# Post-norm attention and ternary FFN layer on eight cores: four 128x128 transposes to a PSUM bank instead of one, and two sets of squaring tiles

## The chip, the cores and the metric

The kernel runs on the 8 cores of one Trainium2 chip, one batch element of 2048 tokens by 2048 features on each core, with no traffic between the cores. The metric is the device time of the slowest core in microseconds. The profile is that of core 0, the slowest in the profiled execution.

## The reference

```python
x = _layernorm(x + attn(x, w_qkv, b_qkv, w_out, b_out))     # x: (8, 2048, 2048) float32
x = _layernorm(x + ffn(x, w_fc, w_proj))
# attn: one head of width 2048
#   qkv = x @ w_qkv.T + b;  scores = q @ k.T / sqrt(2048);  probs = softmax(scores)
#   out = (probs @ v) @ w_out.T + b_out
# ffn:  h = square(relu(x @ ternary(w_fc).T));  out = h @ ternary(w_proj).T     # hidden width 5120
```

Every float32 operand of a matmul is split into a bf16 high part and a bf16 low part (the rest). A product of two split matrices is three bf16 matmuls; one with a ternary matrix is two.

## The kernel before

The program is written out by hand as a list of instructions for each engine. `B.op` appends an instruction to an engine's list with the semaphore values that it waits for; each instruction of VectorE, ScalarE and GpSimd also waits for the completion of the one before it on its own engine. So each engine works its list strictly in order.

First come the transposes of x (L337 to L344) and then the QKV projection (L484) with the ternary quantization of the FFN weights beside it. The V part of this stage ends in `v_emit`: four transposes (L439) of 128x128 into the four quarters of one PSUM bank, then four 128-column evictions on each of ScalarE (L445) and VectorE (L452).

Then four groups `g` of 512 tokens run one after the other, each through these stages:

1. scores: matmuls L649, copies of 8 PSUM banks to `sco` (L667, L671);
2. softmax and the transposes of the probabilities, for each of 4 row tiles `qt` (a row tile is 128 tokens): row maximum (L690), bias (L694), exponential with the row sum (L697), reciprocal (L702), normalization (L704), then 16 steps `kc`, each with one float32 transpose of 128x128 on TensorE (L710) into the first 128 columns of PSUM bank 0 or 1 in turn, a ScalarE copy of these to bf16 in `pth` (L714), and a VectorE subtraction for the low part in `ptl` (L718), which frees the bank;
3. probabilities times V: matmuls L760, evictions L773 and L777;
4. output projection: matmuls L831, L842, L845, residual added by L849;
5. first layer norm, for each of 4 row tiles `sci`: sum (L861), sum of squares (L866), small steps (L864 to L880), application (L882), then again 16 steps of transpose (L900), high part (L904, in `y1fh`) and low part (L907, in `y1fl`), with PSUM banks 0 and 1 in turn;
6. first FFN product: 40 accumulations of 32 matmuls (L939); after each, relu into `rl` (L947, ScalarE), its square into `t2` (L950, VectorE), the high part of it (L952, ScalarE) and the low part (L954, VectorE). There is one tile `rl` and one tile `t2`;
7. second FFN product: matmuls L999, evictions L1014, and a second layer norm with the store.

The matmuls of stage 3 wait for the last low part of stage 2 (`t_pt_done[-1]`), those of stage 6 for the last low part of stage 5 (`t_y1_tr[-1]`), and those of stage 7 for the last low part of stage 6 (`t_hsq_done[-1]`). No matmul of another stage is queued between the transposes. A stretch of 16 transposes with their evictions is called a unit below: 4 groups with 4 row tiles at two places make 32 units.

Of the kernel before, what the change touches and what calls it, by code (L numbers as in the profile page):

```python
# [7 lines left out]
AL = mybir.AluOpType  # L8
AF = mybir.ActivationFunctionType
# [84 lines left out]
def build_core():  # L94
# [46 lines left out]
    pb = [nc.alloc_psum_tensor("pb%d" % i, [128, 512], F32).ap() for i in range(8)]  # L141

    B = Builder(nc)
# [26 lines left out]
    for c, v in ((C2048, 2048.0), (CN, 10485760.0), (C7, 7.0), (C10, 10.0),  # L170
# [46 lines left out]
    tern_scale = {}  # L217
# [356 lines left out]
    pth = bb(PTH, 8192)  # L574
# [9 lines left out]
    y1fh = bb(Y1FH, 8192)  # L584
    y1fl = bb(Y1FL, 8192)
    qfcs = bb(QFCS, 8192)
    rl = bf(RL, 512)
    t2 = bf(T2, 512)
# [4 lines left out]
    for g in range(4):  # L593
        s30 = s3_end if g == 0 else []

        def ge(*keys):
            return [grp_end[k] for k in keys]
# [90 lines left out]
        for qt in range(4):  # L688
            pnb = pn2[qt % 2]
            t_nm = B.op("vector", lambda e, qt=qt: e.tensor_reduce(  # L690
                vcol(NMAX), sco[:, qt * 2048:(qt + 1) * 2048], axis=AX.X, op=AL.max,
                negate=True), waits=sco_qt_toks[qt] + [pn_norm[qt % 2]],
                inc="sV")
            t_eb = B.op("vector", lambda e: e.tensor_tensor(  # L694
                vcol(EBIAS), vcol(NMAX), vcol(SSCB), op=AL.mult),
                waits=[t_sscb], inc="sV")
            t_exp = B.op("scalar", lambda e, qt=qt, pnb=pnb: e.activation(  # L697
                pnb, sco[:, qt * 2048:(qt + 1) * 2048], AF.Exp,
                bias=vcol(EBIAS), scale=vcol(SSCB), accum_out=vcol(ESUM)),
                waits=[t_eb, pn_read[qt % 2]] + (ge("pe") if qt == 0 else []),  # L700
                inc="sA")
            t_rq = B.op("vector", lambda e: e.reciprocal(vcol(RQ), vcol(ESUM)),  # L702
                        waits=[t_exp], inc="sV")
            t_pn = B.op("vector", lambda e, pnb=pnb: e.tensor_single_scalar(  # L704
                pnb, pnb, vcol(RQ), op=AL.mult),
                waits=[t_rq], inc="sV")
            pn_norm[qt % 2] = t_pn
            for kc in range(16):
                bk = kc % 2
                t_tr = B.op("tensor", lambda e, kc=kc, bk=bk, pnb=pnb: e.transpose(  # L710
                    pb[bk][:, 0:128], pnb[:, kc * 128:(kc + 1) * 128], idn),
                    waits=[t_pn, bank_free[bk]], inc="sP")
                dst = kc * 512 + qt * 128
                t_hi = B.op("scalar", lambda e, bk=bk, dst=dst: e.activation(  # L714
                    pth[:, dst:dst + 128], pb[bk][:, 0:128], AF.Copy),
                    waits=[t_tr] + (ge("out0", "out1") if qt == 0 and kc == 0 else []),
                    inc="sA")
                t_lo = B.op("vector", lambda e, bk=bk, dst=dst: e.tensor_tensor(  # L718
                    ptl[:, dst:dst + 128], pb[bk][:, 0:128], pth[:, dst:dst + 128],
                    op=AL.subtract), waits=[t_tr, t_hi], inc="sV")  # L720
                bank_free[bk] = t_lo
                t_pt_done.append(t_lo)
            pn_read[qt % 2] = t_tr
# [162 lines left out]

        t_y1_tr = []
        t_ln_prev = None
        for sci in range(4):
            y_toks = [y_map[(sci, oh_, os_)] for oh_ in range(2) for os_ in range(2)]  # L890
            t_ap, _ = layer_norm(
                yb[:, sci * 2048:(sci + 1) * 2048],
                y1b[:, sci * 2048:(sci + 1) * 2048],
                y_toks + [t_qsl_lastread if sci == 0 else None],
                sci, dump_extra=t_y_done[-1] if sci == 0 else None)
            t_ln_prev = t_ap
            for dc in range(16):
                bk = (sci * 16 + dc) % 2
                src_off = sci * 2048 + dc * 128
                t_tr = B.op("tensor", lambda e, src_off=src_off, bk=bk: e.transpose(  # L900
                    pb[bk][:, 0:128], y1b[:, src_off:src_off + 128], idn),
                    waits=[t_ap, bank_free[bk]], inc="sP")
                dst = dc * 512 + sci * 128
                t_hi = B.op("scalar", lambda e, bk=bk, dst=dst: e.activation(  # L904
                    y1fh[:, dst:dst + 128], pb[bk][:, 0:128], AF.Copy),
                    waits=[t_tr], inc="sA")
                t_lo = B.op("vector", lambda e, bk=bk, dst=dst: e.tensor_tensor(  # L907
                    y1fl[:, dst:dst + 128], pb[bk][:, 0:128], y1fh[:, dst:dst + 128],
                    op=AL.subtract), waits=[t_tr, t_hi], inc="sV")
# [5 lines left out]
        t_rl_free = None  # L915
        t_t2_free = None
        for hcb in range(10):
            t_qld = []
            for dc in range(16):
                t_qld.append(B.dma(qfcs[:, dc * 512:(dc + 1) * 512],  # L920
                             qfc[dc * 128:(dc + 1) * 128, hcb * 512:(hcb + 1) * 512],
                             waits=[t_qf_free if dc == 0 else None,
                                    t_d_lastmm if hcb == 0 and dc == 0 else None] +
                             (tern_done[0] if g == 0 and hcb == 0 and dc == 0 else []),
                             stream="ts%d" % dc))
            t_mmf = {}
            for h4 in range(4):
                bk = h4 + 4 * (hcb % 2)
                n_mm = 0
                for dc in range(16):  # L930
                    for amat in (y1fh, y1fl):
                        first = (n_mm == 0)
                        last = (n_mm == 31)
                        w = []
                        if first:
                            w = [t_y1_tr[-1], bank_free[bk]]
                        if h4 == 0 and amat is y1fh:
                            w = list(w) + [t_qld[dc]]
                        t_mmf[bk] = B.op("tensor", lambda e, dc=dc, h4=h4, amat=amat, bk=bk, first=first, last=last: e.matmul(  # L939
                            pb[bk], qfcs[:, dc * 512 + h4 * 128: dc * 512 + h4 * 128 + 128],  # L940
                            amat[:, dc * 512:(dc + 1) * 512],
                            start=first, stop=last),
                            waits=w, inc="sP" if last else None)
                        n_mm += 1
                hca = hcb * 4 + h4
                hoff = hsq_off(hca)
                t_rl = B.op("scalar", lambda e, bk=bk: e.activation(  # L947
                    rl, pb[bk], AF.Relu, scale=vcol(SFCB)),
                    waits=[t_mmf[bk], tern_scale[0], t_rl_free], inc="sA")
                t_t2 = B.op("vector", lambda e: e.tensor_tensor(t2, rl, rl, op=AL.mult),  # L950
                            waits=[t_rl, t_t2_free], inc="sV")
                t_hi = B.op("scalar", lambda e, hoff=hoff: e.activation(  # L952
                    bb(hoff, 512), t2, AF.Copy), waits=[t_t2], inc="sA")
                t_lo = B.op("vector", lambda e, hoff=hoff: e.tensor_tensor(  # L954
                    bb(hoff + 1024, 512), t2, bb(hoff, 512), op=AL.subtract),
                    waits=[t_hi], inc="sV")
# [120 lines left out]
```

How the kernel before makes its waits and increments, by code:

```python
                    def run(eng):  # L78
                        satisfied = {}
                        for fn, ws, inc in self.ops[eng_name]:
                            for sname, v in ws:
                                if satisfied.get(sname, -1) >= v:
                                    continue
                                eng.wait_ge(handles[sname], v)
                                satisfied[sname] = v
                            ins = fn(eng)
                            if inc is not None:
                                ins.then_inc(handles[inc[0]], inc[1])
```

## Time and profile before

| | us |
|---|---|
| median of the 2 timed runs | 8209.84 (7855.29 and 8564.4) |
| profiled execution, device time | 7726.85 |
| its span on core 0 | 7724.7 |
| spans of its other cores | 7624.6 to 7713.0 |
| TensorE busy on core 0 | 6804.0 (88%) |
| VectorE, ScalarE busy | 1320.9 (17%), 1549.1 (20%) |

The span runs from a core's first instruction to its last. The profiled execution is shorter than both timed runs; a saving found in the trace is one of microseconds in that execution.

### The profile page before, as it was taken

The page shows a single profiled execution, that of the slowest core. Times are in us where ns is not written, and L with a number is a line of the kernel's source. Part 1 is how long each engine was busy: PE and PEld are TensorE (multiplying, and loading weights), DVE is VectorE, ACT ScalarE, POOL GpSimd, SP SyncE. Part 2 cuts the span into 40 slices and gives each one's busy share as a digit, 9 for nine tenths or more (in the row PEclk, how much of TensorE's full clock was granted, in tenths as well). Part 3 has the DMA queues.
Part 4 walks back from the last instruction along what each step waited for, and adds up shares of the span by engine and source line. Part 5 has one row for each costly group of instructions (what it writes and reads, how often), then busy time and mean ns, then how long its engine had stood idle before and what let it go on. Part 6 is the DMA issues. An engine that isn't in the chain of part 4 may idle for free.

```text
span 7724.7 us, 82337 instructions; the slowest of 8 cores (7624.6 to 7724.7 us)
## 1 busy us (share of the span) xinstructions
PE 6804.0 (88%) x29840; PEld 3014.2 (39%) x29840; DVE 1320.9 (17%) x2408; ACT 1549.1 (20%) x2523; POOL 259.3 (3%) x499
## 2 busy tenths in 40 slices
PE   5999998899998798899779799987979998797998
PEld 2344443344444343334334333433433443343343
DVE  3111244312221201210110211011021000202101
ACT  3333566612221101210110111011021000102100
POOL 0111122200000000000000000000000000000000
PEclk9888999999999798899879799997979999797999
DMA  2556777713333132122313112231312223131222
GB/s 99 149 158 175 203 233 235 228 63 94 95 100 106 60 118 79 51 62 75 119 58 119 64 55 69 76 123 58 117 50 66 70 73 129 59 116 46 66 71 82
DMA packets 394272, 785.58 MB, mean 102 GB/s; under 512 B 105105, under 2 KB 219793, under 8 KB 381585
## 3 DMA queue, kind: packets, MB, share of 16 engines
q1 hardware_dynamic: 334994, 570.59, 23.2%
q0 software_dynamic: 58880, 209.75, 9.5%
q8 instruction: 243, 3.98, 0.2%
q14 instruction: 155, 1.27, 0.1%
HBM read 654.34 MB, written 125.83 MB: 101 GB/s over the span
## 4 chain that ended last, share of the span: by engine, by line
PE 77%; ACT 7%; DVE 7%; issue 3%; DMA 3%; SPq 1%; DVEq 0%; ACTq 0%; POOL 0%; POOLq 0%
PE pb L484 20%; PE pb L939 14%; PE pb L999 14%; PE pb L649 9%; PE pb L831 9%; PE pb L760 8%; DVE ab L280 2%; ACT af L274 2%; ACT af L278 2%; DMA ab<-qfc 1%; SPq L61 1%; ACT af L882 1%; PE pb L710 1%; PE pb L337 1%; PE pb L900 1%
## 5 line engine op out<-in xcount | busy, mean ns | idle before, releaser
L484 PE MATMUL pb<-ab,ab 128*128 128x512 bf16 x9216 | 2113.3, 394 | 59.6 <-ACT af L278 44.7
L484 PEld LDWEIGHTS pb<-ab,ab 128*128 128x128 bf16 x9216 | 927.2, 101 | 1220.5 <-issue 379.2
L939 PE MATMUL pb<-ab,ab 128*128 128x512 bf16 x5120 | 1177.1, 390 | 102.0 <-DMA ab<-qfc 95.0
L999 PE MATMUL pb<-ab,ab 128*128 128x512 bf16 x5120 | 1118.3, 381 | 18.8 <-DVE ab L954 14.8
L939 PEld LDWEIGHTS pb<-ab,ab 128*128 128x128 bf16 x5120 | 497.6, 100 | 780.7 <-issue 270.7
L649 PE MATMUL pb<-ab,ab 128*128 128x512 bf16 x3072 | 672.0, 382 | 139.6 <-DMA ab<-qf 139.6
L999 PEld LDWEIGHTS pb<-ab,ab 128*128 128x128 bf16 x5120 | 499.2, 98 | 637.8 <-issue 53.6
L831 PE MATMUL pb<-ab,ab 128*128 128x512 bf16 x3072 | 680.7, 385 | 26.5 <-DVE ab L777 14.1
L760 PE MATMUL pb<-ab,ab 128*128 128x512 bf16 x3072 | 672.0, 382 | 4.6 <-DVE ab L718 4.6
L649 PEld LDWEIGHTS pb<-ab,ab 128*128 128x128 bf16 x3072 | 302.0, 98 | 509.3 <-issue 153.2
L831 PEld LDWEIGHTS pb<-ab,ab 128*128 128x128 bf16 x3072 | 303.4, 99 | 404.0 <-issue 53.3
L760 PEld LDWEIGHTS pb<-ab,ab 128*128 128x128 bf16 x3072 | 302.2, 98 | 373.6 <-issue 17.3
L866 ACT ACTIVATE af<-af 128x2048 f32<-128x2048 f32 x32 | 61.1, 1910 | 1867.7 <-DVE af L1014 1122.8
L900 PE MATMUL pb<-idn,af 128*128 128x128 f32 x256 | 105.7, 444 | 216.3 <-ACT af L882 141.1
L947 ACT ACTIVATE af<-pb,st 128x512 f32<-128x512 f32 x160 | 110.0, 687 | 913.6 <-PE pb L939 913.6
L710 PE MATMUL pb<-idn,af 128*128 128x128 f32 x256 | 105.7, 444 | 206.8 <-DVE af L704 130.4
L950 DVE TENSOR_TENSOR af<-af 128x512 f32<-128x512 f32 x160 | 110.7, 692 | 913.4 <-ACT af L947 913.4
L280 DVE TENSOR_TENSOR ab<-af,af 128x1024 bf16<-128x1024 f32 x160 | 196.0, 1225 | 385.9 <-ACT af L278 325.2
L1014 DVE SCALAR_TENSOR_TENSOR af<-pb,st,af 128x512 f32<-128x512 f32 x64 | 48.0, 750 | 1091.6 <-PE pb L999 1085.8
L274 ACT ACTIVATE af<-af,st 128x1024 f32<-128x1024 f32 x160 | 183.7, 1148 | 211.0 <-DVE ab L280 210.3
L495 ACT ACTIVATE ab<-pb,bqkv_sb 128x512 bf16<-128x512 f32 x128 | 88.0, 687 | 517.6 <-PE pb L484 507.7
L337 PE MATMUL pb<-idn,af 128*128 128x128 f32 x256 | 108.7, 446 | 91.7 <-DVE ab L344 84.0
(89 smaller groups left out, 2628.5 us busy)
## 6 DMA issues: line engine op xcount, KB each, us to landing
af<-wfct POOLq DMA_DIRECT2D x160, 512.0 KB, 5.5
af<-wprt POOLq DMA_DIRECT2D x160, 512.0 KB, 6.0
ab<-qfc SPq DMA_DIRECT2D x640, 128.0 KB, 2.9
ab<-qpr SPq DMA_DIRECT2D x320, 256.0 KB, 2.7
ab<-kf SPq DMA_DIRECT2D x128, 512.0 KB, 3.3
ab<-vt SPq DMA_DIRECT2D x128, 512.0 KB, 3.3
ab<-wos SPq DMA_DIRECT2D x128, 512.0 KB, 3.3
af<-wqk SPq DMA_DIRECT2D x48, 1024.0 KB, 6.7
```

Source lines behind the costliest of these rows:

```text
L274: t_s1 = B.op("scalar", lambda e, b=buf, tc=NTHRv: e.activation(tz_ta, b, AF.Sign, bias=vcol(tc)), waits=[load_tok[k], t_q] + (stats[wi] i ...
L278: t_s2 = B.op("scalar", lambda e, b=buf, tc=THRv: e.activation(tz_tb, b, AF.Sign, bias=vcol(tc)), inc="sA")
L280: t_q = B.op("vector", lambda e, qb=qb: e.tensor_tensor(qb, tz_ta, tz_tb, op=AL.add), waits=[q_free[qsl_], t_s2], inc="sV")
L337: t_tr = B.op("tensor", lambda e, xr=xrow, hc=hc, bk=bk: e.transpose(pb[bk][:, 0:128], xr[:, hc * 128:(hc + 1) * 128], idn), waits=[t_ld, ...
L484: t_mm = B.op("tensor", lambda e, a=a, bmat=bmat, hc=hc, ss=ss, bk=bk, first=first, last=last: e.matmul(pb[bk], a[:, hc * 128:(hc + 1) * 128],
L649: t_hcmm = B.op("tensor", lambda e, a_off=a_off, b_off=b_off, bk=bk, kb=kb, first=first, last=end_of_acc: e.matmul(pb[bk], qsl[:, a_off:a_ ...
L710: t_tr = B.op("tensor", lambda e, kc=kc, bk=bk, pnb=pnb: e.transpose(pb[bk][:, 0:128], pnb[:, kc * 128:(kc + 1) * 128], idn), waits=[t_pn, ...
L760: t_last = B.op("tensor", lambda e, vbuf=vbuf, a_off=a_off, kc=kc, pmat=pmat, bk=bk, first=first, last=end_of_acc: e.matmul(pb[bk], vbuf[: ...
L831: t_last = B.op("tensor", lambda e, amat=amat, coff=coff, wbuf=wbuf, b_off=b_off, bk=bk, first=first: e.matmul(pb[bk], amat[:, coff:coff + ...
L900: t_tr = B.op("tensor", lambda e, src_off=src_off, bk=bk: e.transpose(pb[bk][:, 0:128], y1b[:, src_off:src_off + 128], idn), waits=[t_ap, ...
L939: t_mmf[bk] = B.op("tensor", lambda e, dc=dc, h4=h4, amat=amat, bk=bk, first=first, last=last: e.matmul(pb[bk], qfcs[:, dc * 512 + h4 * 12 ...
L999: t_last = B.op("tensor", lambda e, a_ap=a_ap, sci=sci, qpb=qpb, ds=ds, bk=bk, first=first, last=end_of_acc: e.matmul(pb[bk], a_ap[:, sci ...
```

## The change

In stages 2 and 5 the 16 steps become 4. Each step now makes four transposes into the four quarters of one PSUM bank, with one wait ahead of the first and one semaphore increment behind the last. One ScalarE copy and one VectorE subtraction then take all 512 columns; in `pth`, `ptl`, `y1fh` and `y1fl` they write four runs of 128 elements that lie 512 elements apart. The banks are still 0 and 1 in turn. In stage 6, `rl` and `t2` each get a second tile, at byte offsets 32768 and 34816 (inside `yb`, in the rows of the first row tile), used in turn; the first two relus wait for VectorE's last step of the first layer norm's first row tile as well.

```diff
-    RL, T2 = 163840, 165888
+    RLS = [163840, 32768]
+    T2S = [165888, 34816]
...
-            for kc in range(16):
-                bk = kc % 2
-                t_tr = B.op("tensor", lambda e, kc=kc, bk=bk, pnb=pnb: e.transpose(
-                    pb[bk][:, 0:128], pnb[:, kc * 128:(kc + 1) * 128], idn),
-                    waits=[t_pn, bank_free[bk]], inc="sP")
...
+            for kc4 in range(4):
+                bk = kc4 % 2
+                t_tr = None
+                for j in range(4):
+                    kc = kc4 * 4 + j
+                    t_tr = B.op("tensor", lambda e, kc=kc, j=j, bk=bk, pnb=pnb: e.matmul(
+                        pb[bk][:, j * 128:(j + 1) * 128],
+                        pnb[:, kc * 128:(kc + 1) * 128], idn,
+                        start=(j == 0), stop=(j == 3), is_transpose=True),
+                        waits=[t_pn, bank_free[bk]] if j == 0 else (),
+                        inc="sP" if j == 3 else None)
+                dsth = pth.rearrange("p (kc c) -> p kc c", c=512)[
+                    :, kc4 * 4:kc4 * 4 + 4, qt * 128:qt * 128 + 128]
+                dstl = ptl.rearrange("p (kc c) -> p kc c", c=512)[
+                    :, kc4 * 4:kc4 * 4 + 4, qt * 128:qt * 128 + 128]
+                t_hi = B.op("scalar", lambda e, bk=bk, dsth=dsth: e.activation(
+                    dsth, pb[bk], AF.Copy),
...
+                t_lo = B.op("vector", lambda e, bk=bk, dsth=dsth, dstl=dstl: e.tensor_tensor(
+                    dstl, pb[bk], dsth, op=AL.subtract),
+                    waits=[t_tr, t_hi], inc="sV")
                 bank_free[bk] = t_lo
...
+                pi = hca % 2
+                rl = rls[pi]
+                t2 = t2s[pi]
...
-                    waits=[t_mmf[bk], tern_scale[0], t_rl_free], inc="sA")
+                    waits=[t_mmf[bk], tern_scale[0], t_rl_free[pi]] +
+                    ([ln1_vtok[0]] if hca < 2 else []), inc="sA")
...
-                t_rl_free = t_t2
-                t_t2_free = t_lo
+                t_rl_free[pi] = t_t2
+                t_t2_free[pi] = t_lo
```

The edit of stage 5 is the same as that of stage 2, with `y1b`, `y1fh` and `y1fl` in place of `pnb`, `pth` and `ptl`.

## Rows read from the trace of the kernel before

**Rows 1.** Spans and mean granted TensorE clock by core and die:

```profile
core 0: 7724.7 us, clock 0.921
...
die 1 (median of its cores): 7634.8 us, clock 0.933
```

**Rows 2.** The page's chain that ended last, shares of the span by line:

```profile
PE pb L484 20%; PE pb L939 14%; PE pb L999 14%; PE pb L649 9%; PE pb L831 9%; PE pb L760 8%; DVE ab L280 2%; ACT af L274 2%; ACT af L278 2%; DMA ab<-qfc 1%; SPq L61 1%; ACT af L882 1%; PE pb L710 1%; PE pb L337 1%; PE pb L900 1%
```

**Rows 3.** The chain in order of time, first group: start us, us, what:

```profile
2616.36 0.46 PE pb L710
2617.84 0.46 PE pb L710
...
2628.59 2.30 DVE st L690
...
2635.35 0.46 PE pb L710
...
2686.34 164.26 PE pb L760 x753
...
3049.12 0.46 PE pb L900
...
3061.42 2.30 DVE st L861
```

**Rows 4.** Timeline, first unit: start us, us, engine line op, [idle before, releaser]:

```profile
2616.36 0.66 PE L710 MATMUL pb<-idn,af 128*128 128x128 f32 x2 [9.12 <-DVE af L704]
...
2617.84 0.84 PE L710 MATMUL pb<-idn,af 128*128 128x128 f32 x2 [0.82 <-DVE ab L718]
...
2618.44 0.67 ACT L714 ACTIVATE ab<-pb 128x128 bf16<-128x128 f32 x2 [0.84 <-PE pb L710]
2618.89 0.69 DVE L718 TENSOR_TENSOR ab<-pb,ab 128x128 bf16<-128x128 f32 x2 [0.80 <-ACT ab L714]
...
2619.33 0.84 PE L710 MATMUL pb<-idn,af 128*128 128x128 f32 x2 [0.65 <-DVE ab L718]
```

**Rows 5.** Groups by line: count, busy us, mean ns, idle before and releasers:

```profile
L900 PE MATMUL pb<-idn,af 128*128 128x128 f32 x256 | 105.7, 444 | 216.3 <-ACT af L882 141.1 <-DVE ab L907 75.1
L710 PE MATMUL pb<-idn,af 128*128 128x128 f32 x256 | 105.7, 444 | 206.8 <-DVE af L704 130.4 <-DVE ab L718 76.3
...
L718 DVE TENSOR_TENSOR ab<-pb,ab 128x128 bf16<-128x128 f32 x256 | 74.6, 291 | 124.8 <-ACT ab L714 108.6 <-PE pb L710 3.6 <-DVE ab L718 0.6
...
L714 ACT ACTIVATE ab<-pb 128x128 bf16<-128x128 f32 x256 | 71.1, 278 | 148.3 <-PE pb L710 134.6 <-ACT ab L714 0.4
```

**Rows 6.** The same view, instructions with 512 and 2048 columns:

```profile
L385 ACT ACTIVATE ab<-af 128x2048 bf16<-128x2048 f32 x48 | 91.7, 1910 | 6.8 <-DMA af<-wqk 2.5
...
L849 DVE TENSOR_TENSOR af<-pb,af 128x512 f32<-128x512 f32 x64 | 44.3, 692 | 692.1 <-PE pb L845 686.3
```

**Rows 7.** Timeline of TensorE, four transposes of L439 between matmuls of L484:

```profile
1745.31 0.60 PE L439 MATMUL pb<-idn,af 128*128 128x128 f32 x4
...
1745.75 10.52 PE L484 MATMUL pb<-ab,ab 128*128 128x512 bf16 x48
```

**Rows 8.** Stretches of core 0: busy us of each engine, granted clock, DMA share, GB/s:

```profile
2628.50:2686.00 57.50, 19.70 (x48) 8.50 (x48) 25.58 (x60) 19.88 (x54) 0.00 (x0) 0.50 0.00 1
2686.00:2690.00 4.00, 3.66 (x10) 1.36 (x11) 0.09 (x1) 0.00 (x0) 0.00 (x0) 0.56 0.00 0
2690.00:2696.00 6.00, 6.00 (x30) 2.74 (x28) 0.00 (x0) 0.00 (x0) 0.00 (x0) 1.00 0.25 87
...
3049.00:3119.00 70.00, 26.31 (x64) 11.42 (x64) 28.35 (x85) 30.93 (x76) 0.00 (x0) 0.50 0.00 1
```

**Rows 9.** Groups by line for the squaring chain and the matmuls behind it:

```profile
L999 PE MATMUL pb<-ab,ab 128*128 128x512 bf16 x5120 | 1118.3, 381 | 18.8 <-DVE ab L954 14.8 <-DVE af L1014 2.8 <-DMA ab<-qpr 0.9
...
L954 DVE TENSOR_TENSOR ab<-af,ab 128x512 bf16<-128x512 f32 x160 | 110.8, 693 | 153.8 <-ACT ab L952 153.8
L950 DVE TENSOR_TENSOR af<-af 128x512 f32<-128x512 f32 x160 | 110.7, 692 | 913.4 <-ACT af L947 913.4
...
L947 ACT ACTIVATE af<-pb,st 128x512 f32<-128x512 f32 x160 | 110.0, 687 | 913.6 <-PE pb L939 913.6
...
L952 ACT ACTIVATE ab<-af 128x512 bf16<-128x512 f32 x160 | 100.7, 629 | 162.8 <-DVE af L950 162.8
```

**Rows 10.** Stretches of core 0 in the QKV stage, columns as in Rows 8:

```profile
400.00:600.00 200.00, 193.59 (x737) 80.78 (x736) 28.97 (x73) 69.71 (x110) 24.83 (x48) 0.81 0.58 161
...
2000.00:2200.00 200.00, 200.00 (x966) 95.78 (x964) 41.21 (x85) 48.52 (x105) 0.00 (x0) 1.00 0.35 94
```

More of the change, by code:

```diff
@@ L707, in build_core @@
             pn_norm[qt % 2] = t_pn
-            for kc in range(16):
-                bk = kc % 2
-                t_tr = B.op("tensor", lambda e, kc=kc, bk=bk, pnb=pnb: e.transpose(
-                    pb[bk][:, 0:128], pnb[:, kc * 128:(kc + 1) * 128], idn),
-                    waits=[t_pn, bank_free[bk]], inc="sP")
[L713 to L716, printed above, removed]
+            for kc4 in range(4):
[15 more added lines that the diff above has]
+                    dsth, pb[bk], AF.Copy),
+                    waits=[t_tr] + (ge("out0", "out1") if qt == 0 and kc4 == 0 else []),
                     inc="sA")
-                t_lo = B.op("vector", lambda e, bk=bk, dst=dst: e.tensor_tensor(
-                    ptl[:, dst:dst + 128], pb[bk][:, 0:128], pth[:, dst:dst + 128],
-                    op=AL.subtract), waits=[t_tr, t_hi], inc="sV")
+                t_lo = B.op("vector", lambda e, bk=bk, dsth=dsth, dstl=dstl: e.tensor_tensor(
+                    dstl, pb[bk], dsth, op=AL.subtract),
+                    waits=[t_tr, t_hi], inc="sV")
                 bank_free[bk] = t_lo
@@ L888, in build_core @@
         t_ln_prev = None
+        ln1_vtok = [None] * 4
         for sci in range(4):
@@ L895, in build_core @@
                 sci, dump_extra=t_y_done[-1] if sci == 0 else None)
+            ln1_vtok[sci] = _
             t_ln_prev = t_ap
[L897 to L909, printed above, removed]
+            for dc4 in range(4):
+                bk = (sci * 4 + dc4) % 2
+                t_tr = None
+                for j in range(4):
+                    src_off = sci * 2048 + (dc4 * 4 + j) * 128
+                    t_tr = B.op("tensor", lambda e, src_off=src_off, j=j, bk=bk: e.matmul(
+                        pb[bk][:, j * 128:(j + 1) * 128],
+                        y1b[:, src_off:src_off + 128], idn,
+                        start=(j == 0), stop=(j == 3), is_transpose=True),
+                        waits=[t_ap, bank_free[bk]] if j == 0 else (),
+                        inc="sP" if j == 3 else None)
+                dsth = y1fh.rearrange("p (dc c) -> p dc c", c=512)[
+                    :, dc4 * 4:dc4 * 4 + 4, sci * 128:sci * 128 + 128]
+                dstl = y1fl.rearrange("p (dc c) -> p dc c", c=512)[
+                    :, dc4 * 4:dc4 * 4 + 4, sci * 128:sci * 128 + 128]
+                t_hi = B.op("scalar", lambda e, bk=bk, dsth=dsth: e.activation(
+                    dsth, pb[bk], AF.Copy), waits=[t_tr], inc="sA")
+                t_lo = B.op("vector", lambda e, bk=bk, dsth=dsth, dstl=dstl: e.tensor_tensor(
+                    dstl, pb[bk], dsth, op=AL.subtract),
+                    waits=[t_tr, t_hi], inc="sV")
                 bank_free[bk] = t_lo
@@ L914, in build_core @@
         t_qf_free = None
-        t_rl_free = None
-        t_t2_free = None
+        t_rl_free = [None, None]
+        t_t2_free = [None, None]
         for hcb in range(10):
@@ L946, in build_core @@
                 hoff = hsq_off(hca)
-                t_rl = B.op("scalar", lambda e, bk=bk: e.activation(
+                pi = hca % 2
+                rl = rls[pi]
+                t2 = t2s[pi]
+                t_rl = B.op("scalar", lambda e, bk=bk, rl=rl: e.activation(
                     rl, pb[bk], AF.Relu, scale=vcol(SFCB)),
-                    waits=[t_mmf[bk], tern_scale[0], t_rl_free], inc="sA")
-                t_t2 = B.op("vector", lambda e: e.tensor_tensor(t2, rl, rl, op=AL.mult),
-                            waits=[t_rl, t_t2_free], inc="sV")
-                t_hi = B.op("scalar", lambda e, hoff=hoff: e.activation(
+                    waits=[t_mmf[bk], tern_scale[0], t_rl_free[pi]] +
+                    ([ln1_vtok[0]] if hca < 2 else []), inc="sA")
+                t_t2 = B.op("vector", lambda e, rl=rl, t2=t2: e.tensor_tensor(
+                    t2, rl, rl, op=AL.mult),
+                    waits=[t_rl, t_t2_free[pi]], inc="sV")
+                t_hi = B.op("scalar", lambda e, hoff=hoff, t2=t2: e.activation(
                     bb(hoff, 512), t2, AF.Copy), waits=[t_t2], inc="sA")
-                t_lo = B.op("vector", lambda e, hoff=hoff: e.tensor_tensor(
+                t_lo = B.op("vector", lambda e, hoff=hoff, t2=t2: e.tensor_tensor(
                     bb(hoff + 1024, 512), t2, bb(hoff, 512), op=AL.subtract),
```

4 lines of the change are left out of this document (2 added, 2 removed).

## The prediction

> **What bounds the kernel now.** I read the spans by core first: core 0 is the slowest, die 1 is some 1% shorter at a slightly higher clock [rows 1], so an interval of core 0 stands for all. The chain that ended last belongs to matmuls for the most part [rows 2]: the six large matmul lines have 74% of the span, and the change touches none of them. L710 and L900 have 1% each there, but this understates them, because a unit's chain goes round TensorE, ScalarE and VectorE and only the TensorE piece bears that name. The chain in order of time shows a unit whole. In the softmax it runs from the first transpose at 2616.36 to 2628.59, where VectorE begins the next row tile: 12.23 us; in the layer norm from 3049.12 to 3061.42, 12.30 us [rows 3]. Nothing else runs beside it: the DMA share is 0.00 in both stretches [rows 8], and the matmuls of the next stage wait for the last low part. So 32 units, about 32 x 12.2 = 390 us, 5% of the span, lie bare on the path.
>
> Within a unit the timeline shows a ring of two banks. A pair of transposes starts at 2617.84, the next at 2619.33 [rows 4]: 1.49 us for each of 8 pairs. Its steps are 0.60 us from a transpose's start to its copy's start (2617.84 to 2618.44), 0.45 us from there to the subtraction's start (2618.89), of which 0.278 us is the copy [rows 5] and 0.17 us the hand-over, then 0.291 us of subtraction [rows 5], and 0.15 us until TensorE starts again. TensorE's own work is not the limit; four hand-overs and two short evictions are.
>
> **The change part by part.** It removes 12 of 16 ScalarE copies and 12 of 16 VectorE subtractions in each unit, and adds 384 columns to each of the others. The transposes are as many as before.
>
> The copy: 0.278 us for 128 columns from PSUM [rows 5]. For the slope I take a plain copy to bf16 without pointer operands from SBUF: 0.629 us for 512 columns (L952) [rows 9] and 1.910 us for 2048 (L385) [rows 6], so 1.281 / 1536 = 0.834 ns a column. That gives 0.278 + 384 x 0.000834 = 0.598 us. The nearest upper row is L947, from PSUM with a pointer scale, 0.687 us [rows 9]. I take 0.60.
>
> The subtraction: L849 reads 512 columns of PSUM and as many of SBUF in 0.692 us [rows 6]; I take 0.69. That the four runs of 128 lie 512 elements apart is shown by no row; the least it can cost is nothing, and I take that, since 128 elements in a run is what each instruction writes now.
>
> Four transposes in a row: with the clock at its low level (0.50 through both stretches [rows 8], 1.2 GHz) a pair that nobody holds up lasts 0.66 us, one lasts 0.444 [rows 4, 5], so the second starts 0.21 us behind the first. At the high level L439 starts four in 1745.75 - 1745.31 = 0.44 us [rows 7], 0.11 each; twice that is the same 0.21 or so. So a burst occupies TensorE for 4 x 0.21 = 0.85 us, and the copy starts 0.60 + 3 x 0.21 = 1.24 us behind the first transpose. The other end, in case weight load and matmul don't overlap beyond the first pair, is 0.43 us each, about a transpose's recorded duration of 0.444.
>
> One unit, from its first transpose at 0: T0 0, copy 1.24 to 1.84, subtraction 2.01 to 2.70, bank free and T2 starts 2.85. T1 starts at 0.85, copy 2.09 to 2.69, subtraction 2.86 to 3.55, T3 starts 3.70. T2's copy is at 4.09 to 4.69, its subtraction 4.86 to 5.55. T3's copy is at 4.94 to 5.54, its subtraction 5.71 to 6.40. The next row tile's VectorE work starts 0.10 later, at 6.50, against 12.23: 5.73 us saved. With 32 units that is 183 us. I don't count the 12.30 of the layer norm, nor the shorter distance between the last transposes and the next matmul.
>
> What comes next after a unit is unchanged: from 2628.59 to the next unit's first transpose at 2635.35 TensorE waits 6.76 us for the serial softmax steps, which depend on data and keep their place. So the stretch stays bare. Nothing is late in its place: the DMA queues are idle there [rows 8], and the V rows for L760 and the weights for L939 have landed before the stretches begin.
>
> A rule of the Trainium skill bears on the copy (page "VectorE: DVE Perf Modes", section "The TRN2 errata"): it gives ScalarE from PSUM (172 + columns) cycles at 1.2 GHz, which is 250 ns for 128 columns where the row shows 278, and 570 ns for 512, an estimate from that page. With it a unit would be some 0.06 us shorter and the sum about 2 us larger; the sum goes by the rows.
>
> The two squaring sets: the chain of an accumulation is 0.687 + 0.692 + 0.629 + 0.693 = 2.70 us plus hand-overs, and ScalarE sits idle for 913.6 / 160 = 5.7 us before each L947, waiting for TensorE [rows 9]. With one tile or two, `rl` is long free when the next accumulation ends. I cost this at 0; what hides it is the accumulation's own matmuls. If that cover were gone, it would be the end of the stage, where L999 waits 14.8 / 4 = 3.7 us for L954 [rows 9]: that is the one last chain, whose steps depend on each other, and a second tile doesn't shorten it. A gain is excluded there, and a loss too, as the added wait on the first layer norm is over some 60 us before the first relu, and on ScalarE nothing else is queued.
>
> Sum: 7726.85 - 183 = 7544 us against the profiled execution's own time, 2.4% less. The timed runs shown are longer, median 8209.84, so the same execution's level is 6% under them. The same 183 us off that median would give 8027, and 2.2%.
>
> **The rivals.**
>
> A, transposes that don't stream at 0.21. At 0.43 us each, copies start 1.88 behind the first transpose, a burst takes 1.71, T2 starts at 3.49, T3 at 5.20, the last subtraction ends 5.20 + 1.88 + 0.60 + 0.17 + 0.69 = 8.54. The saving is 3.59 a unit, 115 us: 7612, within 2%. For it: no row shows more than two in a row at the low clock, and the recorded duration is 0.444. Against it: L439's four in 0.44 us. Dearer strided writes would have a like effect: 0.7 us more in each unit is enough to fall below 2%.
>
> B, the clock comes up within a unit. It rises about 4 us into L760's dense matmuls and stands at 1.00 in the next stretch, after 0.50 through the transposes [rows 8], where TensorE started two of 0.21 in each 1.49 us. Now four of 0.21 stand in each 1.4 us or so. At 2.4 GHz I estimate a burst's copy to start 0.48 us sooner: 3 x 0.10 for the spacing, and some 0.17 for the last transpose (0.60 - 3 x 0.11 = 0.27 in place of 0.444 [rows 5, 7]). Once in each unit (T2 and T3 only) that is 15 us; the eight matmul stages behind then don't start with 4 us at half speed, 8 x 2 = 16 us more. That gives 7544 - 31 = 7513. If every burst were fast, the unit would be 5.55 and the whole saving 226: 7501. Against it: 7 us without transposes still lie between units.
> The Trainium skill (page "TensorE: Matmul & The Clock Gate", section "The HAM clock gate") states that the clock rises on sustained activity and falls after idleness; by that rule too the outcome hangs on how full the bursts are, and the trace agrees on the rise of about 4 us.
>
> C, slower: the chip grants less clock elsewhere. Between 400 and 600 us core 0 has 0.81, and only 737 matmuls are done there against 966 at 1.00 [rows 10]. If units that are denser made this state hold in the matmul stages as well, each microsecond of dense matmul would cost 1 / 0.81 - 1 = 0.23 more. It eats the 183 us from 183 / 0.23 = 800 us of such matmuls on, and gives over 2% slower from 1470 us on: 7544 + 0.23 x 1500 = 7889. For it: the state is there in this execution. Against it: it is not there in any of the four groups, where the change is.
>
> D, nothing: each burst waits for the one before it to be evicted whole, and a unit is 4 x 2.85 = 11.4 us, with 0.8 saved in each: 7700. Against it: pairs overlap now, with the same two banks.
>
> **How the numbers follow.** Forecast 0.58, A with its like 0.20, B 0.13, C 0.05, D 0.04. 2% is about what a measurement of this kernel can tell from no change, 155 us here. The forecast lies only 28 us beyond that line, so a tenth of it counts as within 2%: faster 0.52 + 0.13 = 0.65, same 0.06 + 0.24 = 0.30, slower 0.05. In the profiled execution's terms the range is 7500 (B at its full) to 7612 (A), and that is the forecast's own range. Executions of one kernel differ more than that: the timed runs of before lie at 7855 and 8564. A time taken as their median was would be 8027 with the forecast. The stated range reaches from 7490 to 8040 to hold both.
>
> **What the profile would show.** The step L710 to L690 in the chain goes from 12.23 to 6.5 us; 64 copies of 128x512 at each place take 598 ns each (right) or 687; 64 subtractions take 692 ns; four transposes start within 0.64 us of each other (right) or 1.3 (A); the granted clock in the two stretches is 0.50 (right) or above 0.6 (B); L999 still waits about 15 us for L954. The prediction is wrong if matmul stages change their granted clock, or if writes in four runs cost more than writes in one.

## The result

Over all executions the changed kernel has a median of 8125.93 us (11 executions, 7462.28 to 8562.94) and the kernel before one of 8450.11 us (10, 7646.0 to 8742.89). Put against each other without the executions in which a die was held at a lower TensorE clock for a long time, the ratio is 0.977 with a 95% interval of 0.970 to 0.984: 2.3% less time. The interval lies wholly below 1, so the gain is real; a gain of a little under 2% is not excluded by it. The forecast was 2.4% less. The time of 8125.93 lies above the stated range of 7490 to 8040.

The profiled execution of the changed kernel took 7472.31 us, 72 us less than the 7544 forecast for it. Its spans by core (from first to last instruction, with the mean granted clock):

```profile
core 0: 7455.0 us, clock 0.945
...
core 7: 7470.8 us, clock 0.942
die 0 (median of its cores): 7448.2 us, clock 0.945
die 1 (median of its cores): 7458.9 us, clock 0.943
```

Against [rows 1] core 0 is 270 us shorter but die 1 only 176 us. The difference between these two is not the change: in the profile of before core 0 had a granted clock of 0.81 for 481 us of its QKV matmuls ([rows 10] show a part of them), and in this one it had none of that. At 0.81 instead of 1.00 some 90 of these 481 us are lost, which is about the 94 us of difference.

A unit in the changed kernel, from the timeline of core 7 (start us, us, engine line op, idle before and releaser). L714 are the transposes, L724 the copies, L728 the subtractions, L691 the next row tile's maximum:

```profile
2542.67 1.94 PE L714 MATMUL pb<-idn,af 128*128 128x128 f32 x8 [9.12 <-DVE af L705]
2543.91 0.60 ACT L724 ACTIVATE ab<-pb 128x512 bf16<-128x512 f32 x1 [3.22 <-PE pb L714]
2544.68 0.69 DVE L728 TENSOR_TENSOR ab<-pb,ab 128x512 bf16<-128x512 f32 x1 [2.27 <-PE pb L714]
2544.76 0.60 ACT L724 ACTIVATE ab<-pb 128x512 bf16<-128x512 f32 x1 [0.26 <-PE pb L714]
...
2545.51 1.94 PE L714 MATMUL pb<-idn,af 128*128 128x128 f32 x8 [0.90 <-DVE ab L728]
...
2548.38 0.69 DVE L728 TENSOR_TENSOR ab<-pb,ab 128x512 bf16<-128x512 f32 x1 [0.16 <-DVE ab L728]
2549.17 2.29 DVE L691 TENSOR_REDUCE st<-af 128x1 f32<-128x2048 f32 x1
```

The first copy starts 1.24 us behind the first transpose, the third burst 2.84 us behind the first, and the next row tile's work at 6.50 us, where the ring of [rows 3, 4] had 12.23. The first layer norm has the same shape: 2959.29 to 2965.79, 6.50 us too, against 12.30.

The groups by line of the changed kernel (count, busy us and mean ns, idle before and releasers) that answer to [rows 5, 6, 9]:

```profile
L1023 PE MATMUL pb<-ab,ab 128*128 128x512 bf16 x5120 | 1114.4, 380 | 19.3 <-DVE ab L978 14.8 <-DVE af L1038 2.8 <-DMA ab<-qpr 1.3
...
L914 PE MATMUL pb<-idn,af 128*128 128x128 f32 x256 | 62.1, 424 | 164.6 <-ACT af L892 150.1 <-DVE ab L926 14.5
L714 PE MATMUL pb<-idn,af 128*128 128x128 f32 x256 | 62.1, 424 | 153.3 <-DVE af L705 138.5 <-DVE ab L728 14.8
...
L728 DVE TENSOR_TENSOR ab<-pb,ab 128x512 bf16<-128x512 f32 x64 | 44.3, 692 | 61.5 <-PE pb L714 51.8 <-ACT ab L724 4.8 <-DVE ab L728 4.5
...
L724 ACT ACTIVATE ab<-pb 128x512 bf16<-128x512 f32 x64 | 38.2, 597 | 81.1 <-PE pb L714 80.6
```

TensorE's idle time for a bank (behind L728 and L926) went from 76.3 and 75.1 us to 14.8 and 14.5. The wait of the second FFN product for the last low part is 14.8 us, as before.

The granted clock in the first group's two stretches and in the matmuls that follow them (us from the span's start, the stretch, busy us and count of PE, PEld, DVE, ACT and POOL, clock, DMA share, GB/s):

```profile
2542.67:2589.10 46.43, 15.53 (x64) 12.01 (x65) 22.76 (x28) 16.11 (x22) 0.00 (x0) 0.50 0.00 0
2589.10:2593.00 3.90, 3.90 (x10) 1.39 (x11) 0.00 (x0) 0.00 (x0) 0.00 (x0) 0.50 0.01 4
2593.00:2598.00 5.00, 5.00 (x24) 2.24 (x23) 0.00 (x0) 0.00 (x0) 0.00 (x0) 0.96 0.09 16
2959.29:3006.06 46.77, 15.53 (x64) 12.01 (x65) 20.79 (x37) 22.72 (x28) 0.00 (x0) 0.50 0.00 0
```

Still 0.50, 1.2 GHz, throughout: the denser bursts did not bring the clock up. The softmax stretch went from 69.98 us (2616.36 to 2686.34 [rows 3]) to 46.43, the one of the layer norm from 70.04 (3049.12 to 3119.16) to 46.77. These are 23.55 and 23.27 us; times four groups, 187 us.

A measure that leaves the QKV stage out is the time from a core's first score matmul to its end. It serves for all comparisons below. The first start stands in the row of that matmul's line (ns min/median/max, first and last start), here of core 0 in the changed kernel and of core 0 before:

```profile
L650 PE MATMUL pb<-ab,ab x3072: 376/379/634, 2361.4 to 6355.9; 128*128 128x512 bf16 x192
```

```profile
L649 PE MATMUL pb<-ab,ab x3072: 376/379/634, 2439.0 to 6574.1; 128*128 128x512 bf16 x192
```

So core 0 needs 7455.0 - 2361.4 = 5093.6 us for its four groups, and needed 7724.7 - 2439.0 = 5285.7. The medians over the eight cores are 5091.0 and 5284.9: 193.9 us less. On die 1 alone they are 5095.4 and 5283.5, 188 us less; in before's median over all eight there are two cores, 2 and 3, with 5350, whose clock was at 0.81 near their end.

### The profile page after: what moved, and what is told of

Same layout as the page of the kernel before. It is cut to its first block, busy times and chain, and to the rows that moved or that the text cites. A ratio compares the mean times of both kernels' runs of the same rounds, so it can differ in the third digit from the quotient of the medians.

```text
span 7470.8 us, 79265 instructions; the slowest of 8 cores (7443.9 to 7470.8 us)
## 1 busy us (share of the span) xinstructions
PE 6629.6 (89%) x29840; PEld 2999.6 (40%) x29840; DVE 1261.0 (17%) x2024; ACT 1483.4 (20%) x2139; POOL 258.2 (3%) x499
## 4 chain that ended last, share of the span: by engine, by line
PE 77%; ACT 7%; DVE 7%; DMA 4%; issue 3%; SPq 1%; DVEq 0%; ACTq 0%; POOL 0%; POOLq 0%
PE pb L484 19%; PE pb L958 14%; PE pb L1023 14%; PE pb L841 9%; PE pb L650 9%; PE pb L770 9%; DVE ab L280 2%; ACT af L274 2%; ACT af L278 2%; DMA ab<-qfc 1%; SPq L61 1%; ACT af L892 1%; PE pb L337 1%; DMA qpr<-ab 1%; PE pb L914 1%
## 5 line engine op out<-in xcount | busy, mean ns | idle before, releaser
L484 PE MATMUL pb<-ab,ab 128*128 128x512 bf16 x9216 | 2033.5, 383 | 63.7 <-ACT af L278 42.0
L484 PEld LDWEIGHTS pb<-ab,ab 128*128 128x128 bf16 x9216 | 908.5, 99 | 1163.5 <-issue 124.6
L958 PE MATMUL pb<-ab,ab 128*128 128x512 bf16 x5120 | 1170.0, 388 | 109.2 <-DMA ab<-qfc 98.3
L1023 PE MATMUL pb<-ab,ab 128*128 128x512 bf16 x5120 | 1114.4, 380 | 19.3 <-DVE ab L978 14.8
L650 PE MATMUL pb<-ab,ab 128*128 128x512 bf16 x3072 | 672.6, 382 | 145.7 <-DMA ab<-qf 142.5
L841 PE MATMUL pb<-ab,ab 128*128 128x512 bf16 x3072 | 683.6, 386 | 30.9 <-DMA ab<-wos 17.1
L770 PE MATMUL pb<-ab,ab 128*128 128x512 bf16 x3072 | 671.8, 382 | 7.5 <-DVE ab L728 7.5
L274 ACT ACTIVATE af<-af,st 128x1024 f32<-128x1024 f32 x160 | 183.7, 1148 | 216.6 <-DVE ab L280 215.9
L914 PE MATMUL pb<-idn,af 128*128 128x128 f32 x256 | 62.1, 424 | 164.6 <-ACT af L892 150.1
L714 PE MATMUL pb<-idn,af 128*128 128x128 f32 x256 | 62.1, 424 | 153.3 <-DVE af L705 138.5
L337 PE MATMUL pb<-idn,af 128*128 128x128 f32 x256 | 108.6, 446 | 90.9 <-DVE ab L344 84.3
L278 ACT ACTIVATE af<-af,st 128x1024 f32<-128x1024 f32 x160 | 183.7, 1148 | 15.4 <-ACT af L274 0.7
```

Of the source, the lines that this page charges most:

```text
L274: t_s1 = B.op("scalar", lambda e, b=buf, tc=NTHRv: e.activation(tz_ta, b, AF.Sign, bias=vcol(tc)), waits=[load_tok[k], t_q] + (stats[wi] i ...
L278: t_s2 = B.op("scalar", lambda e, b=buf, tc=THRv: e.activation(tz_tb, b, AF.Sign, bias=vcol(tc)), inc="sA")
L337: t_tr = B.op("tensor", lambda e, xr=xrow, hc=hc, bk=bk: e.transpose(pb[bk][:, 0:128], xr[:, hc * 128:(hc + 1) * 128], idn), waits=[t_ld, ...
L484: t_mm = B.op("tensor", lambda e, a=a, bmat=bmat, hc=hc, ss=ss, bk=bk, first=first, last=last: e.matmul(pb[bk], a[:, hc * 128:(hc + 1) * 128],
L650: t_hcmm = B.op("tensor", lambda e, a_off=a_off, b_off=b_off, bk=bk, kb=kb, first=first, last=end_of_acc: e.matmul(pb[bk], qsl[:, a_off:a_ ...
L770: t_last = B.op("tensor", lambda e, vbuf=vbuf, a_off=a_off, kc=kc, pmat=pmat, bk=bk, first=first, last=end_of_acc: e.matmul(pb[bk], vbuf[: ...
```

## The experiments

The theory: the whole gain is the shorter ring in the 32 units; the two sets of squaring tiles do nothing. One table for both kernels and the seven variants that bear on it. "Unit" is the first softmax unit of the first group unless said otherwise; "groups" is the median over the cores of the time from the first score matmul to the end; "less" is against the kernel before.

| kernel | unit, us | groups, us | less, us | expected less |
|---|---|---|---|---|
| before | 12.23 | 5284.9 | | |
| changed | 6.50 | 5091.0 | 193.9 | 183 |
| batched transposes only | 6.50 | 5092.4 | 192.5 | 183 |
| two squaring sets only | 12.23 | 5284.2 | 0.7 | 0 |
| bank of four, small evictions | 10.38 | 5223.4 (die 0) | 61.5 | 60 |
| single transposes, eight banks | 7.37 | 5124.9 | 160.0 | 153 |
| changed, four banks | 5.31 | 5048.6 | 236.3 | 183 + 37 = 220 |
| changed, fillers | 6.50, later 5.53 | 5095.8 | 189.1 | 183 + 20 = 203 |
| changed, a row tile ahead | period 7.46 | 4923.9 | 361.0 | 183 + 144 = 327 |

### The change in two halves

```diff
-    RLS = [163840, 32768]
-    T2S = [165888, 34816]
+    RLS = [163840, 163840]
+    T2S = [165888, 165888]
...
-                pi = hca % 2
+                pi = 0
```

> Only the transposes are batched; one rl and one t2 tile as before. Theory (the whole gain is the shorter ring of transpose, copy and subtraction): 6.50 us a unit in both places, as in the changed kernel, and a ratio of 0.977 to the kernel before. Rival (the second set of squaring tiles has a part in it): part of the 176 us is missing here and L999's wait for L954 or the idle time in the first FFN product is longer than in the changed kernel.

The other half is the kernel before with only these lines of the change taken in.

> Only the two sets of squaring tiles; single transposes as before. Theory: 12.23 us a unit, a ratio of 1.00 to the kernel before within 0.3%, and 3.7 us of waiting for the last low part in each group. Rival: up to 1% faster through the first FFN product.

With the batched transposes alone a unit is 6.50 us and the groups take 5092.4 us; with the two sets alone 12.23 and 5284.2. The first half has all of the gain, the second none: 0.7 us is below what differs from core to core. The end of the first FFN product waits as long in both (the first row is of the half with the batched transposes, the second of the one with the two sets):

```profile
L1022 PE MATMUL pb<-ab,ab 128*128 128x512 bf16 x5120 | 1175.2, 395 | 17.2 <-DVE ab L977 14.8 <-DVE af L1037 2.1 <-DMA ab<-qpr 0.2
```

```profile
L1007 PE MATMUL pb<-ab,ab 128*128 128x512 bf16 x5120 | 1117.4, 380 | 19.5 <-DVE ab L962 14.8 <-DVE af L1022 2.6 <-DMA ab<-qpr 1.4
```

### What in the ring costs: hand-overs or evictions

```diff
-                t_hi = B.op("scalar", lambda e, bk=bk, dsth=dsth: e.activation(
-                    dsth, pb[bk], AF.Copy),
...
+                for j in range(4):
+                    dst = (kc4 * 4 + j) * 512 + qt * 128
+                    t_hi = B.op("scalar", lambda e, bk=bk, dst=dst, j=j: e.activation(
+                        pth[:, dst:dst + 128], pb[bk][:, j * 128:(j + 1) * 128], AF.Copy),
...
```

(The subtraction and the layer norm's pair are cut up in the same way. The four subtractions of a bank start when the last of its four copies is done.)

> Four transposes to a bank as in the changed kernel, but four 128-column copies and four 128-column subtractions for each bank (the same columns in all). Theory (each small eviction pays its own start and its wait for the one before it, 0.37 us a copy and 0.40 a subtraction): a unit of 10.3 us, some 60 us less than the kernel before, ratio 0.992. Rival (what costs is the hand-over between engines, four of them instead of sixteen): a unit of about 6.5 us and the full gain of 176 us, ratio 0.977.

The chain in order of time of its slowest core (start us, us, what) starts a unit at 2924.73 and the next row tile at 2935.11, 10.38 us:

```profile
2924.73 1.10 PE pb L714 x4
2925.97 0.29 ACT ab L726
2926.34 0.29 ACT ab L726
...
2927.53 0.30 DVE ab L732
2927.92 0.30 DVE ab L732
...
2935.11 2.30 DVE st L691
```

The hand-overs between engines are as few as in the changed kernel, yet two thirds of the gain are gone. The copies start 0.37 us apart and the subtractions 0.39, for 0.28 and 0.29 us of work: each has its own start and its wait for the one before. The rival fell: in a ring of two banks, few hand-overs alone are not enough. Small evictions in which a subtraction starts as soon as its own copy is done were not tried. Its profile has die 1 at a lower clock for long stretches, so the table takes die 0.

```diff
-                bk = kc % 2
+                bk = kc % 8
...
-                bk = (sci * 16 + dc) % 2
+                bk = (sci * 16 + dc) % 8
```

> The kernel before with nothing changed but the PSUM banks of the transposes: all eight in turn instead of two. Theory (the ring over two banks keeps the engines apart; with eight, VectorE runs one subtraction each 0.40 us): a unit of 0.60 + 0.45 + 15 x 0.40 + 0.29 + 0.10 = 7.4 us, 153 us less, ratio 0.980. Rival (the number of instructions is what counts, not the ring): the unit stays above 11 us.

The unit was 7.37 us: in the chain the transposes start at 2537.21, VectorE runs one subtraction each 0.40 us, and the next row tile starts at 2544.58.

```profile
2537.21 3.92 PE pb L710 x14
2541.12 0.28 ACT ab L714
...
2543.39 0.30 DVE ab L718
2543.79 0.30 DVE ab L718
2544.19 0.30 DVE ab L718
2544.58 2.30 DVE st L690
```

So 160 of the 194 us are to be had by two numbers, with no batching at all. This unit has as many copies and subtractions as the one with small evictions above and is 3 us shorter, so the number of evictions costs what it does there only through the two banks. What held the kernel before was that two banks let only two evictions be under way; the change took both ways at once, in that a bank now holds four transposes.

### Banks on top of the change

```diff
-                bk = kc4 % 2
+                bk = kc4 % 4
```

> The changed kernel with banks 0 to 3 in turn instead of 0 and 1, so that no burst waits for a bank. Theory: T3's copy starts at 2.55 + 1.24 = 3.79, its subtraction ends at 5.25, a unit of 5.35 us instead of 6.50: 32 x 1.15 = 37 us less than the changed kernel, ratio 0.972 to the kernel before. Rival (VectorE or ScalarE is already the limit): a unit of 6.3 us or more.

The first unit runs from 2575.08 to 2580.39, 5.31 us, and the groups are 42 us shorter than the changed kernel's (37 expected):

```profile
2575.08 2.81 PE pb L714 x12
...
2578.80 0.70 DVE ab L728
2579.59 0.70 DVE ab L728
2580.39 2.30 DVE st L691
```

### The price of the clock

```diff
             pn_read[qt % 2] = t_tr
+            for dmy in range(26):
+                B.op("tensor", lambda e: e.matmul(
+                    pb[7], qsl[:, 0:128], qsl[:, 0:512], start=True, stop=True),
+                    waits=[bank_free[7]] if dmy == 0 else ())
```

> The changed kernel with 26 matmuls of 128x512 put behind the transposes of each softmax unit; they write a bank that nobody reads, so they add work and leave the result as it is. It prices the clock. Theory (the bursts run at the low clock because TensorE has idled): from the second unit on a granted clock of 1.00, bursts of four in 0.44 us, a unit of 5.6 us instead of 6.5 at 12 to 16 places, and the matmuls of probabilities times V start at full clock; some 20 us less than the changed kernel. Rival (the clock has no part): unit 6.5 us, no gain, and a loss if the fillers run into the next unit.

The second unit goes from 2568.16 to 2573.69, 5.53 us, at a clock of 1.00: its copy starts 0.79 us behind the first transpose instead of 1.24. The third began at the high clock and lost it in its second half. Timeline of TensorE:

```profile
2568.16 1.07 PE L714 MATMUL pb<-idn,af 128*128 128x128 f32 x8 [2.10 <-DVE af L705]
...
2571.81 5.78 PE L735 MATMUL pb<-ab 128*128 128x512 bf16 x26
2580.45 1.06 PE L714 MATMUL pb<-idn,af 128*128 128x128 f32 x8 [2.87 <-DVE af L705]
2582.84 1.94 PE L714 MATMUL pb<-idn,af 128*128 128x128 f32 x8 [1.32 <-DVE ab L728]
...
2597.38 6.41 PE L735 MATMUL pb<-ab 128*128 128x512 bf16 x26
2603.62 6.64 PE L774 MATMUL pb<-ab,ab 128*128 128x512 bf16 x30
```

Half of the theory held: the clock is worth about 1 us in a unit that has it throughout (6.50 to 5.53) and about half of that where it is lost midway (the third unit, 2580.45 to 2586.49, took 6.04). The gain did not come: 5095.8 against 5091.0 us. The reason stands in the last two rows. I had put fillers behind the fourth unit as well, and these 26 stand ahead of L774 in TensorE's order. From the unit's last burst, which starts about 2596.5, the evictions take until about 2599.2; the matmuls start at 2603.62. That is over 4 us lost in each group, 17 in all. It outweighs what a group wins: some 2 us in its second to fourth units, and some 2 us in the first matmuls of L774, which no longer start at half speed. A version without the last fillers was not tried.

### The next row tile ahead of this one's evictions

```diff
+        sm_max(0)
+        sm_exp(0)
+        sm_max(1)
         for qt in range(4):
...
+            if qt < 3:
+                sm_exp(qt + 1)
+            if qt < 2:
+                sm_max(qt + 2)
...
-                bk = kc4 % 2
+                bk = (qt * 4 + kc4) % 8
```

(`sm_max` and `sm_exp` are the lines L690 to L697 of before, with their own columns for bias and sum by parity. The first layer norm is split in the same manner: sums and square root of the next row tile are issued between this one's evictions, the application behind them.)

> The batched transposes over eight banks, and the maximum, exponential, sums and layer norm steps of the next row tile issued ahead of this one's evictions, in the softmax and in the first layer norm. Theory (the 6.8 us between units are serial only through the order of issue; VectorE's 7.3 us a row tile are the limit then): a period of 7.3 us a row tile instead of 13.3, some 6 x 3 x 8 = 144 us less than the changed kernel, ratio 0.957 to the kernel before. Rival (VectorE and ScalarE wait for each other in turn as before): a period of 10 us or more, under 80 us gained.

Timeline of core 3, two periods of the softmax; L727 are the transposes, L693 the maximum, L741 the subtractions:

```profile
2553.41 3.65 PE L727 MATMUL pb<-idn,af 128*128 128x128 f32 x16 [9.16 <-DVE af L714]
...
2555.87 3.08 DVE L741 TENSOR_TENSOR ab<-pb,ab 128x512 bf16<-128x512 f32 x4
...
2559.33 1.29 DVE L714 TENSOR_SCALAR af<-af,st 128x2048 f32<-128x2048 f32 x1
...
2560.72 2.29 DVE L693 TENSOR_REDUCE st<-af 128x1 f32<-128x2048 f32 x1
...
2560.87 3.65 PE L727 MATMUL pb<-idn,af 128*128 128x128 f32 x16 [3.80 <-DVE af L714]
```

The period is 7.46 us instead of 13.26 (2542.67 to 2555.93 in the changed kernel), and VectorE has no gap but the 0.1 us or so between two of its instructions. The groups take 4923.9 us: 167 less than the changed kernel's and 361 less than before's. The profiled execution took 7308.21 us; the shortest of before on the same chip was 7668.43, and 7308 / 7668 = 0.953 (one execution of each; the other five of this version took 7833.71 to 8250.71). The time of the groups, over eight cores, says the same more firmly: this version beats both kernels.

### What the long executions hang on

The last question is not on the change but on the level, where the stated range failed. In the changed kernel's executions one die often has its spans near 7440 us with a mean clock of 0.945, while the other has 7800 to 8560 with 0.89 down to 0.80. In the profile of the kernel with small evictions die 1 was such a one, and its QKV matmuls show where: first core 4 of that kernel, then core 0 (columns as above), both between 1600 and 1800 us.

```profile
1600.00:1800.00 200.00, 200.00 (x763) 82.84 (x762) 23.16 (x22) 21.25 (x23) 0.54 (x1) 0.81 0.15 45
```

```profile
1600.00:1800.00 200.00, 199.00 (x935) 94.22 (x953) 36.57 (x64) 41.02 (x79) 0.00 (x0) 1.00 0.29 81
```

763 matmuls in 200 us instead of 935, with TensorE busy throughout.

The kernel before's own profile has such stretches in two places. Core 0 first, then core 2, each over the same two stretches:

```profile
223.00:715.00 492.00, 485.59 (x1849) 201.75 (x1848) 68.52 (x169) 174.36 (x275) 60.87 (x116) 0.81 0.59 160
7186.00:7677.00 491.00, 470.23 (x2110) 204.39 (x2109) 44.77 (x64) 36.86 (x56) 0.00 (x0) 0.98 0.23 70
```

```profile
223.00:715.00 492.00, 482.94 (x2197) 220.37 (x2240) 82.99 (x203) 211.37 (x334) 73.25 (x140) 0.99 0.62 196
7186.00:7677.00 491.00, 463.26 (x1731) 190.10 (x1764) 40.46 (x61) 27.75 (x39) 0.00 (x0) 0.80 0.18 58
```

Cores 0 and 1 are at 0.81 early, in the QKV stage, and cores 2 and 3 for as long near their end, in the FFN products of the last group. So the low clock is not bound to one stage, nor to all four cores of a die at the same place of their programs.

```diff
-    h=whi: e.activation(h, w, AF.Copy),
+    h=whi: e.activation(h, w, AF.Copy, scale=0.0),
...
-            l, w, h, op=AL.subtract),
+            l, w, h, op=AL.mult),
```

> The changed kernel with the bf16 parts of the QKV weights made zero (the copy is scaled by 0, the low part multiplied by it), so every instruction is there and q, k, v and the attention's matmuls work on zeros; the attention's result is left out by this, the FFN works on real data. It asks what the stretches at a clock of 0.81 hang on, which make the long executions of both kernels. Theory (they come with what the matmuls compute: a limit on power): none at 0.81 in the QKV stage, and all executions within 2% of 7460 us, against a kernel before that goes on to spread from 7650 to 8700. Rival (they come with how densely the cores issue matmuls): the spread is as wide as the changed kernel's, 7460 to 8560.

All six executions lie between 7448.49 and 7469.35 us, while the kernel before, on the same chip and between them, went from 7635.57 to 8558.96. The ratio is 0.9725, interval 0.967 to 0.978. No core of the profile had a stretch at 0.81. The groups take 5083 us, 8 less than the changed kernel's, so zeros don't make the instructions themselves faster. So zeros in the attention part are enough to keep the 0.81 away, and dense issue alone does not bring it about; the rival fell. (The changed kernel with real data was not run on this chip; the kernel before stands in for it.) The page's row of the granted clock over the span, in tenths, has its 8s only in slices with one of the 32 units or with the wait at the start of a group, where it is 0.50 as well (0.53 and 0.50 from 3600 to 3640 us):

```profile
PEclk9999999999999898999889899988989998898999
```

The Trainium skill (page "TensorE: Matmul & The Clock Gate", in its note on the peak-current limiter) says that a die goes down to 1.95 GHz (0.81 of 2.4) once three of its cores run dense matmuls, that this depends on the data, and that all-zero operands don't bring it about. The 0.81 and the effect of the zeros agree with it. Whether three cores of a die ran dense matmuls at the same moment can't be read here, because each core's trace counts from its own first instruction.

What starts the low clock in one execution and not in the next stays open, but the profiles hold a pattern. In three of them the two pairs of a die's cores have it at opposite ends of their spans, for about as long: 223 to 715 and 7186 to 7677 us in the kernel before; 254 to 1119 on cores 2 and 3 and 6827 to 7535 on cores 0 and 1 with the batched transposes only; 221 to 2919 on cores 4 and 5 and 5219 to 7943, with breaks, on cores 6 and 7 with the small evictions. The kernel with four banks has the opposite ends too, 222 to 499 and 7269 to 7388, but not the like length. That is what would be seen if one pair began while the other was finishing, and the clock fell while both were at work. The executions would then be longer by as much as the pairs overlap. It is not shown: the traces have no common clock, and stretches of some 160 us from 802 us on, on both pairs of a die at the same place (in the kernel with two squaring sets, for one), don't fit it. That in the run with zeros the FFN kept its clock on real data doesn't say that the FFN is safe from it: in the kernel before cores 2 and 3 had 0.81 there.

## Why the prediction was right and where it failed

**The unit: right to a hundredth.** The mechanism, the ring over two banks, was right. Forecast 6.50 us from the first transpose to the next row tile, measured 6.50. Each term held: the copy 0.598 forecast and 0.597 measured, the subtraction 0.69 and 0.692, the first copy 1.24 behind the first transpose in both, the third burst at 2.85 and 2.84. That four runs of 128 cost what one run costs was an assumption. The subtraction shows it, 692 ns as L849 took with one run; for the copy no row has a plain copy from PSUM in one run of 512 to bf16, and its 597 ns is what the working from one-run rows gave. To the hundredth is better than such terms deserve: 0.15 and 0.17 us of hand-over were read from one place each.

**The sum: 183 us forecast, 194 us measured** on the part behind the QKV stage, and 176 us between the spans of die 1. Two terms were left out on purpose, the longer units of the layer norm and the short end of each stretch. The first group's stretches give 187 us for all, and the cores of die 1 show 188 in their groups. The last 6 us of the 194 lie within what the same part differs by between cores of one kernel, 10 us and more. Die 1's span shows less than its groups do because its QKV stage was some 13 us longer in the profile of after.

**The squaring tiles: right**, shown by the two halves of the change.

**Rival A** (0.43 us between transposes) **and B** (a rising clock) didn't happen: the bursts take 0.21 a transpose and the clock stays at 0.50. What B would be worth was sized at 0.95 us a unit and measured at 0.97 (6.50 to 5.53) where fillers forced it. Two of the rivals' sums don't come out of their own terms: B at its full is 32 x (12.23 - 5.55) + 16 = 230 us and not 226, and it takes 0.9 us more in each unit, not 0.7, to fall below 2%. Neither moves the forecast. **Rival D** is contradicted by the start of the second burst, 0.85 us behind the first. **Rival C** named the right mechanism in the wrong role: the 0.81 clock is the largest thing in the times of both kernels, and both have it, so the change isn't needed to bring it about. What was said against it, that it is in none of the four groups, holds for core 0 alone: cores 2 and 3 had it in their last group (5350 us for the groups, against 5284).

**The range failed, in its last step.** I took the level of a median from two executions, 8209.84, less 183, and ended the range at 8040. Ten executions of the kernel before have a median of 8450, and single ones reach 8743. The medians, 8450.11 and 8125.93, lie 324 us apart, of which the change is 183 to 194; the rest is which executions happened to be long. With 8450 the same subtraction would have given 8267, still 141 us from the measured time. With rival C I had the row for it, 737 matmuls at 0.81 against 966 at 1.00 [rows 10], and priced it as something the change may cause. It should have been read as something that the kernel before already has by itself, worth up to some 0.23 us for each microsecond of the 5700 us (74% of the span [rows 2]) of its large matmuls, an estimate of 1300 us; the longest execution of before in the first ten is 1100 us above the shortest. A range for a time then has to reach to about 8600 (the changed kernel went to 8562.94); one for the ratio could have been narrow.

**The same thing was in the starting time.** "An interval of core 0 stands for all" is true of the intervals, but not of the sum: the 7726.85 us from which 183 were taken held the 481 us at 0.81 on core 0. Die 1 had next to none of it, and its 7634.8 less 183 is 7452; it measured 7458.9. So the forecast of 7544 for the profiled execution was 72 us too long, though its difference was right.

**The reading of "what comes next" was right but stopped too early.** I noted that the 6.8 us between units stay because the steps depend on data. Within a row tile they do, between row tiles they don't: the version with a row tile ahead wins 167 us, most of it by their order (it has more banks as well, worth 42 us where they alone were changed).

## What to carry to other kernels

Follow one round of a ring between engines by its starts, and ask which of its parts recur for each piece: here TensorE was bound by the number of free banks, and either more banks or fewer, larger evictions takes most of the gain. Then look at what the engines do between the rounds, since steps that are serial within a tile can be issued a tile ahead. When a few executions of one kernel differ by ten percent, forecast the difference in microseconds and the ratio, and let a range for the absolute time cover the whole spread of the kernel's executions.

## What the runs showed of the hardware

- The granted clock of 0.81 depends on the operands' values. The changed kernel with zero weights in the attention ran six times within 21 us; on the same chip the kernel before, with real data, went from 7635.57 to 8558.96 us in eleven executions.
- It comes to two neighbouring cores together: in the profile of before to cores 0 and 1 from 223 to 715 us, and to cores 2 and 3 of the same die from 7186 to 7677 us of their own spans.
- The granted clock stayed at 0.50 over the whole stretch of four units, in the kernel before and in the changed one (46.43 us in the softmax). With 26 matmuls of 512 columns in the gap between two units it was 1.00 in the second unit, and in the third it fell back to 0.50 midway.
- A copy of 512 columns out of PSUM to four runs of 128 took 597 ns, one of 128 columns 278 ns; the subtraction 692 and 291 ns. The subtraction paid nothing for the distance between the runs: L849, with one run, took 692 ns too.
- Float32 transposes of 128x128 follow each other at 0.21 us at the low clock, though each is recorded with 0.42.
